# Attention on one core: the value block cut in two, and scores, score pieces and values put in another order

## The chip, the cores and the metric

The kernel runs on one core of a Trainium2 chip. The metric is the device time of one execution in microseconds. The time before is the median of three runs, and the profile is of one further execution with its own time.

## The reference

The input `x` has 2 batches of 2048 tokens with 256 channels. What is computed, cut to what matters:

```python
xn  = layernorm(x)
q, k, v = split(xn @ w_in.T)            # 16 heads of 16 channels
att = einsum('bhqd,bhkd->bhqk', q, k) / 4
att = where(causal, att, 0.0)           # masked scores are 0, not -inf
att = softmax(att)
x + (att @ v) @ w_out.T + ffn(xn)       # ffn: r * (relu(k)**2 @ W_v.T), token-shifted
```

A masked score is 0 and so still weighs its key with exp(0 - max). The kernel adds these keys by a term of their own, from sums of the values behind each query.

## The kernel before

**Stages.** `stage_tokens` normalises, projects and computes the feed-forward part, and lasts to about 222 us. `stage_attention` is the rest. It goes through 8 groups (2 batches by 4 groups of 4 heads). A group has 4 units (`u`, 512 queries each), and unit `u` has `4 * (u + 1)` key tiles (`kt`, 128 keys each): 40 steps in a group. In the last four steps of a unit (the diagonal) only the queries from `first_query` on count, so that these have 512, 384, 256 and 128 queries.

**One step of TensorE** (`group` of the tensor block, L1193) issues, in this order:

- four score tiles (`score_tile`, L1123; heads 0, 2, 1, 3). A head has 50 rows, and the heads lie alternately in rows 0 to 63 and 64 to 127 of the array. A score tile is called S0 to S3 here. S0 and S2 use the lower rows, S1 and S3 the upper.
- after S0 and after S2 one score piece each (`ops.score_piece`, L324): 128 queries by up to 512 keys of two heads, one matmul in the upper rows and one in the lower. VectorE reduces it to a maximum (`reduce_piece`, L349), for the softmax of a later unit. A piece on the diagonal is narrower (128 to 512 columns) and gets four small mask matmuls (L339). 32 of a group's 80 pieces are such. The pieces have two pairs of PSUM banks (`MRING`).
- after S1 `between_scores` (L1179): in step 1 the masked keys of the unit before (L1155, 32 small matmuls), in step 2 a suffix sum of the values (L1119, L1120), in the last group an output tile (L1175) in many steps.
- after S3 the value block of the key tile two steps earlier (`weigh_values`, L1133, `LAG` is 2): four heads in four column strips of the array, over all 128 rows, in fp32, which makes 8 matmuls in the trace. So step 0 of a unit has the values of the last unit's 256-query tile, step 1 those of its 128-query tile, step 2 those of this unit's tile 0, and the later ones those of its other tiles.

**What waits for what.** The score tiles take turns in three PSUM banks (`SRING` is 3, `bank_of`): the tile three uses later waits for ScalarE's exponential (L1014) of the tile before it in the bank. So S3 waits for the exponential of S0 of its own step. A piece waits for VectorE's reduction of the piece two before it. The values wait for the exponentials, and on the diagonal for GpSimd's mask (L966). Each engine takes its work in the order written out. The order of DMAs on the SP queue (L873) hangs on scores, values and reductions by semaphores and is not touched.

Of the kernel before, what the change touches and what calls it, by code (L numbers as in the profile page):

```python
# [18 lines left out]
CH = 512  # L19
NCH = T // CH  # L20
SUB = CH // P
NT = T // P
GH = 4
NG = H // GH
HW = 32
# [16 lines left out]
PIECE0 = [SUB * (GH // 2) * u * (u + 1) // 2 for u in range(NCH + 1)]  # L42
PIECES = PIECE0[NCH]
# [14 lines left out]
LAG = 2  # L58
NORM_AT = GH * LAG + 1
KT0 = [SUB * u * (u + 1) // 2 for u in range(NCH + 1)]  # L60
# [9 lines left out]
PRING = 16  # L70
SRING = 3
MRING = 2
# [11 lines left out]
def key_tiles(u):  # L84

    return SUB * (u + 1)


def first_query(u, kt):

    return P * max(0, kt - SUB * u)


def spread_pieces():
# [9 lines left out]
def pieces_at(u, kt, half):  # L104

    return SPREAD[u, kt, half], KT0[u] + kt >= AHEAD_FROM
# [14 lines left out]
def bank_of(what, which, G):  # L121

    return (G * len(score_uses()) + score_uses().index((what, which))) % SRING


def rows_of(h, rows):

    return slice(h // 2 * HALF, h // 2 * HALF + rows)
# [664 lines left out]
def stage_attention(nc, block, ops, stores, ident, attn_t, ffn_d, w_out_sb, out):  # L793
# [7 lines left out]
    with ExitStack() as ctx:  # L801
        def sb(name, shape, dt=F32):
            return ctx.enter_context(nc.sbuf_tensor(name, shape, dt))

        def ps(name, shape):
            return ctx.enter_context(nc.psum_tensor(name, shape, F32))

        def sem(name):
            return ctx.enter_context(nc.semaphore(name))

        probs = sb("probs", [P, PRING, CH])
# [8 lines left out]
        ps_m = ps("ps_m", [P, MBANKS, CH])  # L820
        ps_o = ps("ps_o", [P, CH])
# [3 lines left out]
        scores_ready, probs_ready, probs_masked, probs_used = (  # L825
            sem("scores_ready"), sem("probs_ready"), sem("probs_masked"), sem("probs_used"))
# [15 lines left out]
        q_op, k_op, v_sb, after, v_after = ops.q_op, ops.k_op, ops.v_sb, ops.after, ops.v_after  # L842
        keys_after, ones, row_max, shift_loaded, SHIFTS = ops.keys_after, ops.ones, ops.row_max, ops.shift_loaded, ops.SHIFTS
        front_loaded, back_loaded, after_ready, max_ready, shift_ready = (
            ops.front_loaded, ops.back_loaded, ops.after_ready, ops.max_ready, ops.shift_ready)
# [253 lines left out]
        def _(pe):  # L1099
            def wait_for_bank(what, which, i, p, first):  # L1100

                uses = score_uses()
                G = i * 2 + p
                at = uses.index((what, which)) - SRING
                if at < 0:
                    if not first:
                        pe.wait_ge(probs_ready, G * SLOTS + at + 1 + SRING)
                elif uses[at][0] == "scores":
                    pe.wait_ge(probs_ready, G * SLOTS + uses[at][1] + 1 + SRING)
                else:  # L1110
                    pe.wait_ge(v_after_ready, G * 4 + uses[at][1] + 1)
# [11 lines left out]
            def score_tile(u, kt, at, i, p, first, last):  # L1123

                slot = (KT0[u] + kt) * GH + at
                h = HEAD_AT[at]
                rows = rows_of(h, KROWS)
                q0 = first_query(u, kt)
                wait_for_bank("scores", slot, i, p, first)
                pe.matmul(ps_s[:, bank_of("scores", slot, i * 2 + p), 0:CH - q0], k_op[rows, p, h % 2, kt * P:(kt + 1) * P],  # L1130
                          q_op[rows, p, h % 2, u * CH + q0:(u + 1) * CH], start=True, stop=True).then_inc(scores_ready, 1)

            def weigh_values(p, u, kt, G):  # L1133

                n = G * NCH + u
                if kt == 0:
                    pe.wait_ge(sums_ready, n + 1)
                if kt < SUB * u:
                    pe.wait_ge(probs_ready, G * SLOTS + (KT0[u] + kt + 1) * GH + SRING)
                else:  # L1140
                    pe.wait_ge(probs_masked, n * (SUB * GH) + (kt - SUB * u + 1) * GH)
                q0 = first_query(u, kt)
                for at, h in enumerate(HEAD_AT):
                    last = pe.matmul(ps_o[h * HW:(h + 1) * HW, q0:CH], v_sb[:, p, kt, h * HW:(h + 1) * HW],  # L1144
                                     probs[:, ((KT0[u] + kt) * GH + at) % PRING, 0:CH - q0],
                                     start=(kt == 0), stop=(kt == key_tiles(u) - 1))
                last.then_inc(probs_used, 1)

            def masked_keys(p, u, G):

                pe.wait_ge(diag_ready, (G * NCH + u + 1) * DIAGS)
                pe.wait_ge(v_after_ready, G * 4 + u + 1)
                for s in range(SUB):
                    for h in range(GH):
                        last = pe.matmul(ps_o[h * HW:(h + 1) * HW, s * P:(s + 1) * P],  # L1155
                                         v_after[:, p, u * SUB + s, h * HW:(h + 1) * HW],
                                         diag_weight[:, u % 2, h * SUB + s], start=False, stop=False)
                last.then_inc(masked_done, 1)

            def finish_unit(p, u, G, step):  # L1160

                weigh_values(p, u, key_tiles(u) - LAG + step, G)

            def output_tile(k):

# [13 lines left out]
            def between_scores(i, p, u, kt, first, last):  # L1179

                G = i * 2 + p
                nxt = NCH if u == NCH - 1 else 0
                if kt == LAG - 1 and u > 0:
                    masked_keys(p, u - 1, G)
                elif kt == LAG - 1 and not first:
                    masked_keys(1 - p, NCH - 1, G - 1)
                if last and (u, kt) in OUT_AT:
                    output_tile(OUT_AT[u, kt])
                if (u, kt) in SV_AT:
                    wait_for_bank("suffix", SV_AT[u, kt], i, p, first)  # L1190
                    sum_suffix(p, SV_AT[u, kt], G, bank_of("suffix", SV_AT[u, kt], G))

            def group(i, p, first=False, last=False):  # L1193
                G = i * 2 + p
                if not first:
                    pe.wait_ge(front_loaded[p], ops.loaded(p, i + 1))
                    pe.wait_ge(back_loaded[p], ops.loaded(p, i + 1))
                for u in range(NCH):
                    nxt = NCH if u == NCH - 1 else 0
                    pe.wait_ge(shift_loaded[u % 2], (G * (NCH // 2) + u // 2 + 2) * SHIFTS)  # L1200
                    for kt in range(key_tiles(u)):
                        for at in range(GH):
                            score_tile(u, kt, at, i, p, first, last)
                            some, ahead = pieces_at(u, kt, at // 2)
                            if at % 2 == 0 and not (ahead and last):
                                for f in some:
                                    if ahead and f == 0:
                                        pe.wait_ge(front_loaded[1 - p], ops.loaded(1 - p, i + 1 + p))
                                    if ahead and f == PIECE0[NCH // 2]:
                                        pe.wait_ge(back_loaded[1 - p], ops.loaded(1 - p, i + 1 + p))  # L1210
                                    ops.score_piece(pe, ps_m, MRING, f, 1 - p if ahead else p, (G + ahead) * PIECES)
                            if at == GH // 2 - 1:
                                between_scores(i, p, u, kt, first, last)
                            if at == GH - 1:


                                if kt >= LAG:
                                    weigh_values(p, u, kt - LAG, G)
                                elif u > 0:
                                    finish_unit(p, u - 1, G, kt)  # L1220
                                elif not first:
                                    finish_unit(1 - p, NCH - 1, G - 1, kt)
                if last:
                    masked_keys(p, NCH - 1, G)
                    for step in range(LAG):
                        finish_unit(p, NCH - 1, G, step)
                    for k in range(len(OUT_AT), OUTS):
                        output_tile(k)

# [3 lines left out]
            pe.wait_ge(ops.piece_reduced, HEAD_START + MRING)  # L1233
            stores.gates(pe)
            group(0, 0, first=True)
            for i in range(B * CC - 1):
                group(i, 1)
                group(i + 1, 0)
# [29 lines left out]
```

## Time and profile before

| | |
|---|---|
| median of 3 runs | 1095.94 us (1093.55 to 1103.12) |
| profiled execution, own time | 1095.51 us |
| its span, first to last instruction | 1092.7 us |
| TensorE matmul busy (share of span) | 1051.1 us (96%) |
| VectorE busy | 843.1 us (77%) |
| ScalarE busy | 696.0 us (64%) |
| GpSimd busy | 386.3 us (35%) |
| exponentials (L1014) | 1280, 599.9 us busy |
| reductions of pieces (L349, ps_m) | 594, 612.0 us busy |
| value matmuls (L1144) | 2560, 301.8 us busy |

A busy TensorE is not one at its peak: the ends of matmuls are modelled, and two matmuls in different rows of the array overlap in the records. The start times are what is read. `PE` is TensorE's matmul, `PEld` its weight load, `ACT` ScalarE, `DVE` VectorE.

### The profile page before, as it was taken

Reading aid. Unit: us, or ns where it says so; the run is one execution under the profiler, and the core shown is the slowest. Engines: PE = TensorE matmul, PEld = TensorE weight load, DVE = VectorE, ACT = ScalarE, POOL = GpSimd, SP = SyncE. Lnnn points to the kernel's source line nnn. Section 1 sums busy time; section 2 is a strip of 40 time slices with the busy share of each in tenths; the row PEclk is TensorE's granted clock in tenths of the full one; section 3 lists DMA queues with packets and bytes.
Section 4 is the critical chain, followed back from the end, with each engine's and each line's share of the span. In section 5 each row is a group of like instructions: output and inputs, shape, how many; then the busy total and the mean of one; then the engine's idle time right before and its main releaser. Section 6 shows DMA issues by size and latency. Waiting matters only on the chain.

```text
span 1092.7 us, 21861 instructions
## 1 busy us (share of the span) xinstructions
PE 1051.1 (96%) x8064; PEld 535.8 (49%) x8064; DVE 843.1 (77%) x1185; ACT 696.0 (64%) x1487; POOL 386.3 (35%) x945
## 2 busy tenths in 40 slices
PE   5999999999999999999999999999999999999998
PEld 3655555554545454444444444544444445454445
DVE  4667788658889878987898889888988888898213
ACT  2433333247776777777777776777777777777672
POOL 3111211355314532445144424343532453163301
PEclk9999999969999999999999999999999999999999
DMA  3596664455004600460055026303520460002123
GB/s 119 171 270 183 192 215 148 145 80 101 8 9 64 103 7 8 65 107 3 16 101 66 7 29 101 47 7 48 94 36 7 60 107 8 9 20 71 45 82 121
DMA packets 62030, 84.13 MB, mean 77 GB/s; under 512 B 12260, under 2 KB 42212, under 8 KB 60900
## 3 DMA queue, kind: packets, MB, share of 16 engines
q1 hardware_dynamic: 60772, 78.55, 33.3%
q0 software_dynamic: 1152, 4.19, 1.3%
q8 instruction: 63, 1.03, 0.4%
q14 instruction: 43, 0.35, 0.1%
HBM read 44.30 MB, written 34.08 MB: 72 GB/s over the span
## 4 chain that ended last, share of the span: by engine, by line
PE 78%; DVE 15%; issue 3%; ACT 2%; DMA 1%; POOL 1%; SPq 0%; ACTq 0%; DVEq 0%; POOLq 0%
PE ps_s L1130 22%; PE ps_o L1144 22%; DVE part_max L349 10%; PE ps_m L332 9%; PE ps_vr L731 4%; PE ps_qk L722 3%; PE ps_o L1155 3%; PE ps_m L1175 3%; PE ps_m L339 3%; PE ps_xt L765 2%; ACT probs L1014 2%; PE ps_qk L731 2%; PE ps_s L1119 2%; DMA x_in<-x 1%; PE ps_s L1120 1%
## 5 line engine op out<-in xcount | busy, mean ns | idle before, releaser
L1014 ACT ACTIVATE probs<-ps_s 128x512 f32<-128x512 f32 (+3 forms) x1280 | 599.9, 537 | 232.4 <-PE ps_s L1130 226.2
L349 DVE TENSOR_REDUCE part_max<-ps_m 128x2 f32<-128x1024 f32 (+2 forms) x594 | 612.0, 1056 | 115.7 <-PE ps_m L332 89.2
L1130 PE MATMUL ps_s<-q_op,k_op 50*128 50x512 f32 (+3 forms) x1280 | 436.3, 424 | 7.0 <-ACT probs L1014 3.5
L332 PE MATMUL ps_m<-k_op,q_op 48*128 48x512 f32 (+3 forms) x1188 | 344.2, 412 | 13.8 <-DVE part_max L349 12.6
L1130 PEld LDWEIGHTS ps_s<-q_op,k_op 50*128 50x128 f32 x1280 | 208.7, 186 | 298.5 <-ACT probs L1014 228.0
L966 POOL TENSOR_SCALAR_AFFINE_SELECT probs<-probs 128x128 f32<-128x128 f32 x512 | 145.4, 294 | 448.3 <-ACT probs L1014 440.6
L1144 PE MATMUL ps_o<-probs,v_sb 128*32 128x512 f32 (+3 forms) x2560 | 301.8, 544 | 0.0
L332 PEld LDWEIGHTS ps_m<-k_op,q_op 48*128 48x128 f32 x1188 | 169.3, 187 | 41.0 <-DVE part_max L349 37.2
L933 POOL TENSOR_TENSOR diag_weight<-ident,masked_weight 128x256 f32<-128x256 f32 x256 | 150.3, 624 | 40.7 <-ACT masked_weight L987 40.6
L339 PE MATMUL ps_m<-mask,pick 64*128 64x64 bf16 (+1 forms) x932 | 97.7, 209 | 0.0
L1144 PEld LDWEIGHTS ps_o<-probs,v_sb 128*32 128x32 f32 x2560 | 50.6, 108 | 71.2 <-ACT probs L1014 33.8
L349 DVE TENSOR_REDUCE part_max<-ps_pieces 128x2 f32<-128x1024 f32 (+3 forms) x46 | 46.5, 1011 | 31.6 <-PE ps_pieces L339 17.7
L722 PE MATMUL ps_qk<-xn_t,w_in_sb 128*128 128x512 f32 x128 | 63.3, 625 | 1.9 <-issue 1.4
L663 ACT ACTIVATE parts<-ps_qk 128x512 fp32r<-128x512 f32 x32 | 19.1, 598 | 71.1 <-PE ps_qk L722 71.1
L523 POOL TENSOR_TENSOR k_act<-k_act 128x1024 f32<-128x1024 f32 x8 | 15.3, 1912 | 119.9 <-ACT k_act L688 119.9
L339 PEld LDWEIGHTS ps_m<-mask,pick 64*128 64x128 bf16 x932 | 47.1, 96 | 14.0 <-issue 1.2
L322 POOL TENSOR_TENSOR after<-after,v_sb 128x64 f32<-128x64 f32 x120 | 39.7, 331 | 8.8
L528 POOL TENSOR_TENSOR ffn<-ffn,x_in 128x512 f32<-128x512 f32 x16 | 21.5, 1346 | 49.8 <-DVE ffn L596 49.8
L722 PEld LDWEIGHTS ps_qk<-xn_t,w_in_sb 128*128 128x128 f32 x128 | 23.6, 196 | 26.0 <-issue 24.1
L1155 PE MATMUL ps_o<-diag_weight,v_after 128*32 128x128 f32 x1024 | 35.4, 280 | 0.0
L1175 PE MATMUL ps_m<-w_out_sb,attn_t 128*128 128x256 f32 x128 | 33.3, 397 | 0.0
L1155 PEld LDWEIGHTS ps_o<-diag_weight,v_after 128*32 128x32 f32 x1024 | 26.7, 111 | 11.7 <-POOL diag_weight L933 8.8
(76 smaller groups left out, 680.3 us busy)
## 6 DMA issues: line engine op xcount, KB each, us to landing
parts_d<-parts SPq DMA_DIRECT2D x32, 512.0 KB, 4.7
q_op<-parts_d SPq DMA_DIRECT2D x84, 128.0 KB, 8.0
k_op<-parts_d SPq DMA_DIRECT2D x84, 128.0 KB, 8.2
vpad_d<-v_pad SPq DMA_DIRECT2D x32, 256.0 KB, 3.5
v_sb<-vpad_d SPq DMA_DIRECT2D x8, 1024.0 KB, 5.8
x_in<-x SPq DMA_DIRECT2D x8, 512.0 KB, 4.9
ffn_d<-ffn SPq DMA_DIRECT2D x8, 512.0 KB, 3.2
attn_t<-normed SPq DMA_DIRECT2D x128, 32.0 KB, 2.0
```

The source lines that it names most:

```text
L332: last = pe.matmul(ps_m[:, f % ring * 2 + e, 0:width], self.q_op[rows, p, j, q0:q0 + P], self.k_op[rows, p, j, pc * CH:pc * CH + width], s ...
L339: last = pe.matmul(ps_m[:, f % ring * 2 + e, s * P + k * HALF:width], self.pick16[half, k], self.mask16[half, k, k * HALF:P], start=False, ...
L349: dve.tensor_reduce(both, ps_m[:, bank:bank + 2, 0:width], AX_X, ALU.max).then_inc(self.piece_reduced, 1)
L722: last = pe.matmul(ps_qk[:, j % 2], w_in_sb[:, cc, j * P:(j + 1) * P], xn_t[:, cc, 1:CH + 1], start=(cc == 0), stop=(cc == CC - 1))
L731: last = pe.matmul(psum[:, s], lhs[:, cc, t * P:(t + 1) * P], weights[:, cc], start=(cc == 0), stop=(cc == CC - 1))
L933: pool.tensor_tensor(diag_weight[:, u % 2, some], ident[:].unsqueeze(1).broadcast_to([P, GH * SUB // DIAGS, P]), masked_weight[:, u, some] ...
L966: pool.affine_select(out=blk, in_=blk, compare_op=ALU.is_ge, fill=0.0, base=0, pattern=[[1, P]], channel_multiplier=-1).then_inc(probs_mas ...
L1014: act.activation(probs[:, slot % PRING, 0:width], ps_s[:, bank_of("scores", slot, i * 2 + p), 0:width], ACT.Exp).then_inc(probs_ready, 1)
L1130: pe.matmul(ps_s[:, bank_of("scores", slot, i * 2 + p), 0:CH - q0], k_op[rows, p, h % 2, kt * P:(kt + 1) * P], q_op[rows, p, h % 2, u * CH ...
L1144: last = pe.matmul(ps_o[h * HW:(h + 1) * HW, q0:CH], v_sb[:, p, kt, h * HW:(h + 1) * HW], probs[:, ((KT0[u] + kt) * GH + at) % PRING, 0:CH ...
L1155: last = pe.matmul(ps_o[h * HW:(h + 1) * HW, s * P:(s + 1) * P], v_after[:, p, u * SUB + s, h * HW:(h + 1) * HW], diag_weight[:, u % 2, h ...
L1175: last = pe.matmul(ps_m[:, k % MBANKS, 0:C], attn_t[:, b * CC + cc, c * CH + t * P:c * CH + (t + 1) * P], w_out_sb[:, cc], start=(cc == 0) ...
```

## The change

The value block is cut into two parts by queries. Part 0 is the columns up to 256 and part 1 the columns from 256. A block of key tile 0, and one whose first query is 256 or later, stays whole and is part 1. The order of a step, which was S0, piece, S1, between, S2, piece, S3, values, is now read from the string `ORDER`: S0, S1, piece, between, values part 0, S2, S3, piece, values part 1. The semaphore that says that a block's probabilities are used is raised by part 1. The other engines' programs are the same.

```diff
+ORDER = "SSMXASSMB"
+
+def weighed_columns(u, kt, part):
+    q0 = first_query(u, kt)
+    if kt == 0 or q0 >= CH // 2:
+        return (q0, CH) if part == 1 else None
+    return (q0, CH // 2) if part == 0 else (CH // 2, CH)
...
-            def weigh_values(p, u, kt, G):
+            def weigh_values(p, u, kt, G, part):
                 n = G * NCH + u
+                if weighed_columns(u, kt, part) is None:
+                    return
...
                 q0 = first_query(u, kt)
+                q1, q2 = weighed_columns(u, kt, part)
                 for at, h in enumerate(HEAD_AT):
-                    last = pe.matmul(ps_o[h * HW:(h + 1) * HW, q0:CH], v_sb[:, p, kt, h * HW:(h + 1) * HW],
-                                     probs[:, ((KT0[u] + kt) * GH + at) % PRING, 0:CH - q0],
+                    last = pe.matmul(ps_o[h * HW:(h + 1) * HW, q1:q2], v_sb[:, p, kt, h * HW:(h + 1) * HW],
+                                     probs[:, ((KT0[u] + kt) * GH + at) % PRING, q1 - q0:q2 - q0],
                                      start=(kt == 0), stop=(kt == key_tiles(u) - 1))
-                last.then_inc(probs_used, 1)
+                if part == 1:
+                    last.then_inc(probs_used, 1)
...
                     for kt in range(key_tiles(u)):
-                        for at in range(GH):
-                            score_tile(u, kt, at, i, p, first, last)
-                            some, ahead = pieces_at(u, kt, at // 2)
-                            if at % 2 == 0 and not (ahead and last):
...
+                        at = m = 0
+                        for op in ORDER:
+                            if op == "S":
+                                score_tile(u, kt, at, i, p, first, last)
+                                at += 1
+                            if op == "M":
+                                some, ahead = pieces_at(u, kt, m)
+                                m += 1
+                                if not (ahead and last):
...
+                            if op == "X":
                                 between_scores(i, p, u, kt, first, last)
-                            if at == GH - 1:
+                            if op in "AB":
+                                part = "AB".index(op)
                                 if kt >= LAG:
-                                    weigh_values(p, u, kt - LAG, G)
+                                    weigh_values(p, u, kt - LAG, G, part)
```

## Rows read from the trace of the kernel before

**Rows 1.** Waits over the whole run: who waited for whom, us in total, times, longest

```profile
PEld ps_s L1130 <- ACT probs L1014: 228.0, 390, 1.3
PEld ps_m L332 <- DVE part_max L349: 37.2, 72, 0.8
```

**Rows 2.** Busy time by stretch, units 0 and 1: PE, PEld, DVE, ACT, POOL, clock, DMA

```profile
650.55:681.72 31.17, 30.10 (x292) 14.89 (x289) 28.76 (x37) 22.01 (x53) 13.84 (x41) 1.00 0.65 106
```

**Rows 3.** Timeline of one plain step: start us, length us, engine, line, operation [idle before]

```profile
630.44 0.50 PE L1130 MATMUL ps_s<-q_op,k_op 50*128 50x512 f32 x1
...
630.79 0.39 PE L1130 MATMUL ps_s<-q_op,k_op 50*128 50x512 f32 x1
...
631.02 0.39 PE L1130 MATMUL ps_s<-q_op,k_op 50*128 50x512 f32 x1
...
631.04 2.06 ACT L1014 ACTIVATE probs<-ps_s 128x512 f32<-128x512 f32 x4 [0.60 <-PE ps_s L1130]
631.22 2.36 DVE L349 TENSOR_REDUCE part_max<-ps_m 128x2 f32<-128x1024 f32 x2 [1.13 <-PE ps_m L332]
...
631.69 0.18 PEld L1130 LDWEIGHTS ps_s<-q_op,k_op 50*128 50x128 f32 x1 [0.48 <-ACT probs L1014]
...
632.12 1.06 PE L1144 MATMUL ps_o<-probs,v_sb 128*32 128x512 f32 x8
...
633.12 0.49 PE L1130 MATMUL ps_s<-q_op,k_op 50*128 50x512 f32 x1
```

**Rows 4.** Timeline, unit 2: end of step 0 and step 1

```profile
578.49 0.64 PE L1144 MATMUL ps_o<-probs,v_sb 128*32 128x256 f32 x8
...
579.06 0.50 PE L1130 MATMUL ps_s<-q_op,k_op 50*128 50x512 f32 x1
...
579.40 0.40 PE L1130 MATMUL ps_s<-q_op,k_op 50*128 50x512 f32 x1
...
579.73 1.08 PE L1155 MATMUL ps_o<-diag_weight,v_after 128*32 128x128 f32 x32
...
580.74 0.50 PE L1130 MATMUL ps_s<-q_op,k_op 50*128 50x512 f32 x1
...
581.41 0.42 PE L1144 MATMUL ps_o<-probs,v_sb 128*32 128x128 f32 x8
...
581.77 0.50 PE L1130 MATMUL ps_s<-q_op,k_op 50*128 50x512 f32 x1
```

**Rows 5.** Timeline, unit 2: step 2, its second piece 384 wide and masked

```profile
582.44 0.70 PE L1119 MATMUL ps_s<-v_sb,keys_after 128*128 128x256 f32 x2
...
583.50 0.50 PE L1130 MATMUL ps_s<-q_op,k_op 50*128 50x512 f32 x1
...
583.88 0.49 PE L1130 MATMUL ps_s<-q_op,k_op 50*128 50x512 f32 x1
...
584.30 1.06 PE L1144 MATMUL ps_o<-probs,v_sb 128*32 128x512 f32 x8
...
585.30 0.50 PE L1130 MATMUL ps_s<-q_op,k_op 50*128 50x512 f32 x1
```

**Rows 6.** Timeline: S0 of the first step of units 2, 3, 0, 1 and 2

```profile
576.49 0.49 PE L1130 MATMUL ps_s<-q_op,k_op 50*128 50x512 f32 x1
...
607.77 0.50 PE L1130 MATMUL ps_s<-q_op,k_op 50*128 50x512 f32 x1
...
650.56 0.49 PE L1130 MATMUL ps_s<-q_op,k_op 50*128 50x512 f32 x1
...
660.34 0.49 PE L1130 MATMUL ps_s<-q_op,k_op 50*128 50x512 f32 x1
...
681.72 0.50 PE L1130 MATMUL ps_s<-q_op,k_op 50*128 50x512 f32 x1
```

**Rows 7.** Timeline, last group: S2 and S3 as a couple without a piece, then values

```profile
1020.10 0.50 PE L1130 MATMUL ps_s<-q_op,k_op 50*128 50x512 f32 x2
...
1020.53 1.06 PE L1144 MATMUL ps_o<-probs,v_sb 128*32 128x512 f32 x8
```

More of the change, by code:

```diff
@@ L1158, in masked_keys, with finish_unit @@
                 last.then_inc(masked_done, 1)
-            def finish_unit(p, u, G, step):
-                weigh_values(p, u, key_tiles(u) - LAG + step, G)
+            def finish_unit(p, u, G, step, part):
+                weigh_values(p, u, key_tiles(u) - LAG + step, G, part)
             def output_tile(k):
@@ L1201, in group @@
                     for kt in range(key_tiles(u)):
-                        for at in range(GH):
-                            score_tile(u, kt, at, i, p, first, last)
-                            some, ahead = pieces_at(u, kt, at // 2)
-                            if at % 2 == 0 and not (ahead and last):
[L1206 to L1212, printed above, removed]
+                        at = m = 0
@@ new lines, in group @@
+                        for op in ORDER:
[6 more added lines that the diff above has]
+                                if not (ahead and last):
+                                    for f in some:
+                                        if ahead and f == 0:
+                                            pe.wait_ge(front_loaded[1 - p], ops.loaded(1 - p, i + 1 + p))
+                                        if ahead and f == PIECE0[NCH // 2]:
+                                            pe.wait_ge(back_loaded[1 - p], ops.loaded(1 - p, i + 1 + p))
+                                        ops.score_piece(pe, ps_m, MRING, f, 1 - p if ahead else p, (G + ahead) * PIECES)
+                            if op == "X":
@@ L1213, in group @@
                                 between_scores(i, p, u, kt, first, last)
-                            if at == GH - 1:
+                            if op in "AB":
+                                part = "AB".index(op)
                                 if kt >= LAG:
-                                    weigh_values(p, u, kt - LAG, G)
+                                    weigh_values(p, u, kt - LAG, G, part)
                                 elif u > 0:
-                                    finish_unit(p, u - 1, G, kt)
+                                    finish_unit(p, u - 1, G, kt, part)
@@ L1221, in group @@
                                 elif not first:
-                                    finish_unit(1 - p, NCH - 1, G - 1, kt)
+                                    finish_unit(1 - p, NCH - 1, G - 1, kt, part)
                 if last:
@@ L1225, in group @@
                     for step in range(LAG):
-                        finish_unit(p, NCH - 1, G, step)
+                        for part in range(2):
+                            finish_unit(p, NCH - 1, G, step, part)
                     for k in range(len(OUT_AT), OUTS):
```

## The prediction

> **What bounds the kernel now.** I read the timeline of one plain step first, then the table of waits, then the odd steps of a unit, then the starts of whole units.
>
> A plain step takes 2.68 us, from S0 at 630.44 to S0 at 633.12 [rows 3]. Four terms make it up, and they close a ring. S0's exponential starts 0.60 after S0, at 631.04. S3, which wants S0's bank, is let go 0.65 later, at 631.69. The value block follows at 632.12, 0.43 later, and the next S0 1.00 after that [rows 3]. TensorE has no other work before S3: S0 and its piece's first half, the second half and S1 at +0.35, S2 and half of the second piece at +0.58, the other half one couple (0.23) later, +0.81. From there to +1.25 it stands, 0.44 us. The table of waits shows the same over the run, 390 waits of score tiles for an exponential, 228.0 us in all [rows 1]. VectorE needs 2.36 of the step, ScalarE 2.06 [rows 3], so neither bounds a plain step, but both are near.
>
> **What TensorE's orders cost.** Matmuls in opposite row halves go in couples. From rows:
> - Couple behind couple: 0.23 (630.79 to 631.02) [rows 3].
> - The first couple behind a value block: 0.35 (630.44 to 630.79, and 579.06 to 579.40) [rows 3, 4], so 0.12 more.
> - From the start of the last couple to a block over all rows: 0.33 (579.40 to 579.73) [rows 4], so 0.10 more.
> - A value block, until the next score: 1.00 for 512 queries [rows 3], 0.57 for 256 (578.49 to 579.06), 0.36 for 128 (581.41 to 581.77) [rows 4]. Two of 256 cost 0.14 more than one of 512.
>
> So cutting a value block adds 0.14 + 0.12 + 0.10 = 0.36 us of TensorE per step, and one crossing each way. Against this stand 0.44 of standing still, and the lone S3's late load (its 0.43 instead of 0.33).
>
> The Trainium skill (TensorEngine Tiling (Array Packing), Key Properties) says that a change of tiling mode drains TensorE. It gives no price; the 0.10 and 0.12 above are this trace's price for it. If the drain cost nothing, 0.22 of each cut step would be saved, some 50 us of the forecast below.
>
> **The new steps.** A half step is a score couple, a piece couple, a value part: 0.35 + 0.33 + 0.57 = 1.25. A plain step is then 2.50, against 2.68. Does the ring allow it? S3 now starts 1.25 behind S0 at the earliest, and 0.60 + 0.65 = 1.25 is when the bank is free [rows 3]. It just fits. The next S1 wants the exponential of S2, by the same sum 1.25 after S2, and just fits too. VectorE's 2.36 fit in 2.50, and the pieces now come evenly, 1.25 apart, where they came 0.58 and 2.10 apart, so that a burst of its other work pushes TensorE less.
>
> That couples of two scores work is seen in the last group, where S2 and S3 start together and the values follow 0.43 later (0.12 + 0.23 + 0.10 gives 0.45) [rows 7].
>
> Now unit by unit, since the other steps don't gain:
> - **Diagonal steps.** Narrower scores don't shorten a couple that hides a load, and their exponentials were short, so that S3 hardly stood. They now pay 2.50. The last one, with a 384-query block cut 128 and 256, costs 0.35 + 0.33 + 0.36 + 0.35 + 0.33 + 0.57 = 2.29.
> - **Step 0.** Its block stays whole. S3 goes at 1.25 as before, but now the second piece is queued behind it: 1.25 + 0.35 + 0.33 + 0.57 = 2.50.
> - **Step 1.** 0.35 + 0.33, masked keys 1.01 (579.73 to 580.74) [rows 4], 0.35 + 0.33 + 0.36: 2.73. It was 2.71.
> - **Step 2.** The suffix comes at 0.67 and lasts 1.06, S3 goes at 2.11 (581.77 to 583.88) [rows 4, 5], held by S1's exponential as before. Behind it 0.35 + 0.33 + 1.00 give 3.79, against 3.53. In unit 0, where the scores are narrow, 0.68 + 1.06 + 0.35 + 0.33 + 1.00 = 3.42.
>
> Sums, against the lengths between the rows' starts [rows 6]:
> - unit 3: 2.50 + 2.73 + 3.79 + 12 x 2.50 + 2.29 = 41.31, was 42.79
> - unit 2: 9.02 + 8 x 2.50 + 2.29 = 31.31, was 31.28
> - unit 1: 9.02 + 4 x 2.50 + 2.29 = 21.31, was 21.38
> - unit 0: 2.50 + 2.73 + 3.42 + 2.29 = 10.94, was 9.78
>
> A group is 104.87 where it was 105.23: only the 18 plain steps gain, and nearly as much is given back.
>
> **Masked pieces.** Their four small matmuls were mostly under S3's standing. Now they end the piece couple that the value part waits for. The step of rows 5 prices them: with a 384-wide masked piece the block came 0.80 behind S2 (583.50 to 584.30) where a plain pair of couples takes 0.67 (580.74 to 581.41) [rows 4]. So 0.13 at 384 columns; at 0.05 per 128 columns (a quarter of 0.21) this is 0.18, 0.13, 0.08 and 0.03 for the four widths, mean 0.105. Some of it was already paid before, so I take 0.09. 32 such pieces in a group make 2.9 us. The bounds are 0 and 0.13, so 0 to 4.2 us. The group is then +2.5, seven groups +17.5.
>
> **The last group.** Its units 0 and 1 cost +1.1, their masks +0.8. From step 5 of unit 2 it has no pieces: three plain steps become 2.25 (S3 at 1.25, 0.43, 0.57), -0.42 each, -1.3. The 17 cut blocks in steps with an output tile pay the 0.14 of the cut and no more, since the output tile crosses anyway: +2.4. Sum +3.0.
>
> **At nothing.** The parts' semaphore waits: exponentials and masks of two steps earlier are long done. The later signal of used probabilities: four slots deep. The SP and GpSimd queues are as before, and their triggers move with the steps. VectorE's floor: units 0 and 1 hold 28.76 us of VectorE in 31.17 [rows 2]; they become 32.25, so it does not bind.
>
> **Sum.** The profiled execution took 1095.5 (its median of runs is 1095.94, so 0.4 off), plus 17.5 and 3.0 is 1116.0. I forecast 1115.
>
> **Rivals.**
> - **A, the masks are hidden, no change.** Mask matmuls run in one row half while the other still streams, and the 0.13 comes from one step where S3 was held as well. Then a group gives -0.36, and with the last group's +2.2 the time is 1095. TensorE's 37.2 us of waits for VectorE [rows 1], of which the even pieces may free more than I took, push the same way. Against: in rows 5 S3 itself went only 0.38 behind S2, 0.04 later than in a plain pair, so that most of the 0.13 came after it [rows 5]. Chance 0.28.
> - **B, a crossing costs less the second time.** If the new crossing cost half of its 0.36, 0.18 x 28 cut steps x 8 groups is 40 us less: 1075. It decides if value blocks overlap the couples' loads. Against: every block in the rows, wide or narrow, has the same fixed part: 1.00, 0.57 and 0.36 less their columns (0.86, 0.43, 0.21) leave 0.14 to 0.15 [rows 3, 4]. Chance 0.12.
> - **C, S3 breaks its couple.** Ring and order both come to 1.25. If the exponential of S0 ends even slightly later than 1.21 behind S0, S3 starts alone, its load bare, and the second piece, queued behind it, too. The price is 0.12 per cut step (the bare load), 0.12 x 28 x 8 = 27 us: 1142. It decides where ScalarE has other work in the step (the copy of sums, the weights). Chance 0.16.
> - **D, loads don't hide in the same half.** In the rows a load hides behind the couple ahead (0.23, not 0.35) [rows 3]. Were that lost where a piece follows the scores, each of 56 half steps would pay 0.12, 47 us in seven groups: 1162. The Trainium skill (TensorE: Matmul & The Clock Gate, The mechanism) says that a weight load overlaps a matmul in flight only where their row groups differ. The 0.23 speaks against it, for S2 came in the rows that the piece before it had used. Chance 0.04.
>
> My own case has 0.40. **Chances.** About 1% is what a measurement can tell from no change, here 1085 to 1107. Slower: nearly all of my case (0.38), C and D, 0.57. Same: A and the edges, 0.30. Faster: B, 0.13. The range runs from 1087, below A's 1095 by some waits for VectorE, to 1142, C. My case alone is 1105 to 1127 by the masks' bounds.
>
> **What would show it.** A plain step at 2.50 (630.44's successor) with S0 and S1 at one start; value parts of 0.57 at +0.68 and +1.93; fewer and shorter waits of scores for exponentials; the diagonal's last step near 2.29 against 1.79; step 2 near 3.79. The gap from a masked piece to the value part decides between me and A. S2 and S3 with different starts is C. I am wrong altogether if the half step is not 1.25.

## The result, and the profile after

The changed kernel takes 1084.07 us (median of 9, 1083.38 to 1088.56) against 1095.94 (9 runs). The ratio is 0.9898, with an interval of 0.9871 to 0.9925: 1% faster, small but clear of the noise. I had forecast 1115, slower, and a range from 1087.

The profiled execution took 1088.56, the longest of the nine, with a span of 1086.4. Its first masked keys come at 244.10, 2.3 us later than in the profile before; in the kernels below this moves between 239.9 and 244.5, whatever the edit, so that the comparisons go by single steps and by the groups behind it.

Part of this is the clock that TensorE was granted. The table of busy times has it at 0.50 (1.2 of 2.4 GHz) for 20.5 us from 226.1 on, where the attention stage has just begun:

```profile
226.10:246.60 20.50, 19.92 (x123) 10.30 (x123) 11.32 (x14) 9.12 (x23) 12.15 (x31) 0.50 0.74 109
```

In the 4.1 us ahead of it TensorE was busy for 1.9. The profile before has such a stretch of 17.1 us, and e2, e3 and e6 below have one of 6.8; all of them begin between 224 and 232 us. Of the nine runs the three with a mean granted clock of 0.997 took 1083.4 to 1084.5, the two with 0.991 1088.0 and 1088.6. So a few us between two runs can be the clock alone.

First the page, its chain that ended last, by engine and by line:

```profile
PE 86%; DVE 7%; issue 2%; ACT 2%; DMA 2%; POOL 1%; SPq 0%; DVEq 0%; ACTq 0%; POOLq 0%
```

It was TensorE 78% and VectorE 15%. Now the waits of the whole run that answer to [rows 1]:

```profile
PEld ps_s L1141 <- ACT probs L1025: 193.1, 483, 1.9
PEld ps_m L343 <- DVE part_max L360: 5.7, 17, 0.9
```

TensorE's waits for VectorE are down from 37.2 us to 5.7, with pieces that come 1.24 apart. The wait of the scores for an exponential has more entries and less time, and part of it is now the value part in front, which the table puts down to the exponential.

The timeline of a plain step, then three halves with masked pieces, answers to [rows 3]:

```profile
581.98 0.50 PE L1141 MATMUL ps_s<-q_op,k_op 50*128 50x512 f32 x2
582.32 0.40 PE L343 MATMUL ps_m<-k_op,q_op 48*128 48x512 f32 x2
...
582.65 0.64 PE L1158 MATMUL ps_o<-probs,v_sb 128*32 128x256 f32 x8
...
583.22 0.50 PE L1141 MATMUL ps_s<-q_op,k_op 50*128 50x512 f32 x2
...
584.46 0.49 PE L1141 MATMUL ps_s<-q_op,k_op 50*128 50x512 f32 x2
...
586.03 0.41 PE L343 MATMUL ps_m<-k_op,q_op 48*128 48x512 f32 x2
...
586.47 0.64 PE L1158 MATMUL ps_o<-probs,v_sb 128*32 128x256 f32 x8
...
587.38 0.23 PE L343 MATMUL ps_m<-k_op,q_op 48*128 48x128 f32 x2
587.45 0.26 PE L350 MATMUL ps_m<-mask,pick 64*128 64x128 bf16 x4
...
587.64 0.64 PE L1158 MATMUL ps_o<-probs,v_sb 128*32 128x256 f32 x8
```

A half step is 1.24 (581.98 to 583.22 to 584.46), 0.34 + 0.33 + 0.57, where 1.25 was forecast; a plain step is 2.48 where it was 2.68. S0 and S1 start together, and so do S2 and S3. A 512-wide masked piece puts the value part 0.44 behind it instead of 0.33; a 128-wide one, masks and all, 0.26.

The diagonal of unit 2 and its borders, where the forecast went wrong:

```profile
597.20 0.45 PE L1141 MATMUL ps_s<-q_op,k_op 50*128 50x384 f32 x2
597.48 0.40 PE L343 MATMUL ps_m<-k_op,q_op 48*128 48x512 f32 x2
...
599.49 0.39 PE L1141 MATMUL ps_s<-q_op,k_op 50*128 50x256 f32 x2
599.71 0.40 PE L343 MATMUL ps_m<-k_op,q_op 48*128 48x512 f32 x2
...
601.72 0.33 PE L1141 MATMUL ps_s<-q_op,k_op 50*128 50x128 f32 x2
601.88 0.44 PE L343 MATMUL ps_m<-k_op,q_op 48*128 48x512 f32 x2
...
603.77 0.50 PE L1141 MATMUL ps_s<-q_op,k_op 50*128 50x512 f32 x2
```

The second, third and fourth steps of the diagonal start at 597.20, 599.49 and 601.72, and the next unit at 603.77: 2.29, 2.23 and 2.05, not 2.50, 2.50 and 2.29. The piece follows two full scores after 0.34, 384-wide ones after 0.28, 256-wide ones after 0.22, 128-wide ones after 0.16.

By unit (stretches of the table of busy times, here of units 2, 3, 0 and 1) [rows 2, 6]:

```profile
572.98:603.77 30.79, 30.52 (x360) 14.58 (x356) 25.94 (x37) 24.16 (x51) 13.93 (x40) 1.00 0.39 48
603.77:645.13 41.36, 41.01 (x449) 18.19 (x445) 35.84 (x41) 32.81 (x68) 13.89 (x33) 1.00 0.03 7
645.13:655.46 10.33, 10.05 (x122) 5.23 (x118) 9.49 (x15) 6.71 (x18) 4.56 (x17) 1.00 1.03 129
655.46:676.39 20.93, 20.62 (x224) 9.57 (x220) 19.86 (x24) 15.45 (x35) 9.29 (x25) 1.00 0.44 94
```

The four make 103.41 where they made 105.23, so -1.8 a group. From the first to the last group's masked keys, seven groups, it is 726.3 before and 714.2 after, -12.1. The last group gives back 3.6: from its first masked keys to the end 124.55 became 128.13. Together this is 8.5 us, 0.8%. The medians are 11.9 apart; the profiles show no more than 8.5 of it as the new order's, and I take the rest for the clock.

By kind of step, in the mean of the six groups between the first and the last, the change takes 2.65 us off the 18 plain steps of a group and 0.76 off the second and third steps of the diagonals. It adds 0.20 to the four steps 0, 0.82 to the four steps 2 (13.79 to 14.61) and 0.75 to the four last steps (7.47 to 8.22). Steps 1 stay as they were. So it gives back half of what it gains.

### The profile page after: what moved, and what is told of

Its sections match the earlier page's. It is cut to its first block, busy times and chain, and to the rows that moved or that the text cites. A ratio compares the mean times of both kernels' runs of the same rounds, so it can differ in the third digit from the quotient of the medians.

```text
span 1086.4 us, 25445 instructions
## 1 busy us (share of the span) xinstructions
PE 1054.0 (97%) x9856; PEld 525.5 (48%) x9856; DVE 851.4 (78%) x1185; ACT 709.9 (65%) x1487; POOL 385.3 (35%) x945
## 4 chain that ended last, share of the span: by engine, by line
PE 86%; DVE 7%; issue 2%; ACT 2%; DMA 2%; POOL 1%; SPq 0%; DVEq 0%; ACTq 0%; POOLq 0%
PE ps_o L1158 27%; PE ps_s L1141 23%; PE ps_m L343 10%; PE ps_vr L742 4%; DVE part_max L360 3%; PE ps_qk L733 3%; PE ps_o L1170 3%; PE ps_m L350 3%; PE ps_xt L776 2%; PE ps_m L1190 2%; PE ps_qk L742 2%; PE ps_s L1130 2%; ACT probs L1025 2%; DMA x_in<-x 1%; PE ps_s L1131 1%
## 5 line engine op out<-in xcount | busy, mean ns | idle before, releaser
L1025 ACT ACTIVATE probs<-ps_s 128x512 f32<-128x512 f32 (+3 forms) x1280 | 609.6, 533 | 210.4 <-PE ps_s L1141 196.2
L360 DVE TENSOR_REDUCE part_max<-ps_m 128x2 f32<-128x1024 f32 (+2 forms) x594 | 619.7, 1060 | 97.0 <-PE ps_m L343 66.3
L1158 PE MATMUL ps_o<-probs,v_sb 128*32 128x256 f32 (+2 forms) x4352 | 349.9, 393 | 0.0
L1141 PE MATMUL ps_s<-q_op,k_op 50*128 50x512 f32 (+3 forms) x1280 | 330.2, 464 | 10.5 <-ACT probs L1025 9.6
L1141 PEld LDWEIGHTS ps_s<-q_op,k_op 50*128 50x128 f32 x1280 | 141.1, 185 | 271.2 <-ACT probs L1025 193.1
L343 PE MATMUL ps_m<-k_op,q_op 48*128 48x512 f32 (+3 forms) x1188 | 247.7, 376 | 1.0 <-DVE part_max L360 0.4
L1158 PEld LDWEIGHTS ps_o<-probs,v_sb 128*32 128x32 f32 x4352 | 86.1, 108 | 116.6 <-ACT probs L1025 48.6
L343 PEld LDWEIGHTS ps_m<-k_op,q_op 48*128 48x128 f32 x1188 | 125.0, 189 | 5.8 <-DVE part_max L360 5.7
L350 PE MATMUL ps_m<-mask,pick 64*128 64x128 bf16 (+1 forms) x932 | 75.5, 210 | 0.0
L350 PEld LDWEIGHTS ps_m<-mask,pick 64*128 64x128 bf16 x932 | 34.9, 96 | 33.9 <-issue 19.1
```

What stands on the lines that cost most here:

```text
L343: last = pe.matmul(ps_m[:, f % ring * 2 + e, 0:width], self.q_op[rows, p, j, q0:q0 + P], self.k_op[rows, p, j, pc * CH:pc * CH + width], s ...
L350: last = pe.matmul(ps_m[:, f % ring * 2 + e, s * P + k * HALF:width], self.pick16[half, k], self.mask16[half, k, k * HALF:P], start=False, ...
L360: dve.tensor_reduce(both, ps_m[:, bank:bank + 2, 0:width], AX_X, ALU.max).then_inc(self.piece_reduced, 1)
L1025: act.activation(probs[:, slot % PRING, 0:width], ps_s[:, bank_of("scores", slot, i * 2 + p), 0:width], ACT.Exp).then_inc(probs_ready, 1)
L1158: last = pe.matmul(ps_o[h * HW:(h + 1) * HW, q1:q2], v_sb[:, p, kt, h * HW:(h + 1) * HW], probs[:, ((KT0[u] + kt) * GH + at) % PRING, q1 - ...
```

## The experiments

Each is the changed kernel with one edit, unless it says otherwise. The order of a step is a string: S a score tile, M a piece, X what stands between, A and B the value parts, V the whole block. Ratios are to the kernel before, in runs on the same chip. "Seven groups" is the stretch from the first to the last group's masked keys in the profile: it leaves the start and the last group out. It begins in unit 1 of the first group and ends in unit 0 of the last, so that it is 10 us short of seven whole groups. e6 is the change itself up to the last group, and has 712.9 where the change has 714.2: a difference of 1.3 in this figure says nothing.

**e1_order_only**

```diff
-ORDER = "SSMXASSMB"
+"SSMXSSMV"      # V: the whole block
```

> Only the order: S0, S1, piece, between, S2, S3, piece, and the value block whole behind it. If the gain came from the order alone, this is as fast as the change, about 1084. By my terms it can't be: S3 still waits until 1.25 behind S0, and the second piece and the whole block are now queued behind it: 1.25 + 0.35 + 0.33 + 1.00 = 2.93 for a plain step against 2.68. 0.25 in 18 plain steps, some 0.25 in the diagonal's first two and in steps 0 and 2, make about 6.5 us a group: near 1145.

Measured: 1146.69, ratio 1.0492 (1.0422 to 1.0562); seven groups 772.9. As expected to 2 us, with plain steps of 2.90 to 3.01 in its profile where 2.93 was summed. The order without the cut is 5% slower, because S3 waits and everything stands behind it.

**e2_cut_only**

```diff
-ORDER = "SSMXASSMB"
+"SMSXSMSAB"     # the order before, both parts behind S3
```

> Only the cut: the order before, with both value parts side by side behind S3. The ring S0, exponential, S3, values is closed as before with 1.14 in place of 1.00: a plain step 2.82, 28 cut blocks a group, 0.14 each, 31 us in all: near 1127. If a cut block cost nothing of itself, 1096.

Measured: 1095.09, ratio 1.0031 (1.0001 to 1.0061); seven groups 726.3, as before. I had 1127. Timeline of its plain step:

```profile
636.50 1.07 PE L1161 MATMUL ps_o<-probs,v_sb 128*32 128x256 f32 x16
637.50 0.18 PEld L1143 LDWEIGHTS ps_s<-q_op,k_op 50*128 50x128 f32 x1 [0.41 <-ACT probs L1027]
```

Sixteen matmuls of 256 columns take the 1.00 that eight of 512 took. That both profiles have 726.3 is partly chance, since the one before has 3 us of half clock in it and e2 none; the five groups from the third on take 526.3 against 525.2. That is 0.2 a group where I had put 3.9. So the 0.14 is not a price of cutting. It is the third part of a crossing, paid once for each stay in the column strips. The sum of a half step was right, since it has one such stay. The 0.14 for an output tile's step was right too, since each part has a stay of its own there, but I had called it by the wrong name.

**e3_couples_before**

```diff
-ORDER = "SSMXASSMB"
+"SMSXASMSB"     # score and piece in a couple, as before
```

> The old couples with the cut between them: S0, piece, S1, between, part 0, S2, piece, S3, part 1. Theory 1 (what counts is that a half step holds two couples and half a block, 1.25): plain steps 2.48 as in the change; steps 0 and 2 keep their second piece ahead of the waiting S3 and stay at 2.4 and 3.5; but narrow scores share their couple with a full piece, so that the diagonal's steps are 2.5, 2.5, 2.3 and not 2.3, 2.2, 2.05. Group 102.6 without masks, near 1080. Theory 2 (the two scores side by side are what gains): near 1095. A masked piece is here followed by its scores, as in rows 5, and may cost up to 0.09 each, 20 us: then near 1100.

Measured: 1082.06, ratio 0.99 (0.9868 to 0.9932), no different from the change; seven groups 711.9 against 714.2. Theory 1 holds: what gains is a half block per half step, not which tiles lie side by side. Its plain steps without a masked piece take 2.48, as in the change. That the whole comes out the same is chance: in the mean of six groups its steps 0 and 2 are 1.6 a group shorter than the change's, and its plain and diagonal steps 1.4 longer. Its masked pieces, in the timeline:

```profile
622.53 0.50 PE L1143 MATMUL ps_s<-q_op,k_op 50*128 50x512 f32 x1
622.54 0.44 PE L345 MATMUL ps_m<-k_op,q_op 48*128 48x384 f32 x1
622.82 0.23 PE L352 MATMUL ps_m<-mask,pick 64*128 64x128 bf16 x1
622.87 0.34 PE L345 MATMUL ps_m<-k_op,q_op 48*128 48x384 f32 x1
...
623.32 0.64 PE L1161 MATMUL ps_o<-probs,v_sb 128*32 128x256 f32 x8
...
626.37 0.50 PE L1143 MATMUL ps_s<-q_op,k_op 50*128 50x512 f32 x1
...
627.22 0.64 PE L1161 MATMUL ps_o<-probs,v_sb 128*32 128x256 f32 x8
...
635.15 0.38 PE L1143 MATMUL ps_s<-q_op,k_op 50*128 50x256 f32 x1
...
635.71 0.64 PE L1161 MATMUL ps_o<-probs,v_sb 128*32 128x256 f32 x8
```

From the first score to the values a plain half has 0.66 to 0.67. With a masked piece 384 wide it has 0.79, 512 wide 0.85. These are the 0.13 and 0.18 of the prediction: the price was right for this order, where a score comes behind the piece, and wrong for the change, where the piece stands last. And with 256-wide scores the half has 0.56, though each score shares its couple with a full piece. I expected narrow scores to save nothing here; that was wrong too.

**e4_after_no_masks**

```diff
-                             ..., start=True, stop=(pc < u))
-        if pc == u:
+                             ..., start=True, stop=True)
+        if False:      # the four mask matmuls of a diagonal piece
```

> The changed kernel without the mask matmuls of the diagonal pieces (their maxima are over unmasked scores). The prediction priced a masked piece at 0.09, 2.9 us a group, which makes about 21 us with the last group's eight: near 1063. The trace after shows gaps from piece to values that are longer by 0.11, 0.04, 0.07 and shorter by 0.07, mean 0.04; but the narrow couples stay narrow without their masks, so leaving out gives back the whole 0.11 per piece only where nothing else holds the step. Theory now: the masks themselves cost about 0.10, and the narrow width had paid back 0.08 of it.

Measured: 1067.64, ratio 0.9766 (0.9712 to 0.982); seven groups 698.6, 15.6 less than with masks: 0.07 for each of 224 masked pieces. 1063 was too low by 5 us.

**e5_before_no_masks** (the same edit in the kernel before)

> The kernel before without the mask matmuls. If S3's standing covered them, as the prediction says, at most 3 us less than before: 1093 to 1096. If they were paid before as well, 10 or more less.

Measured: 1084.83, ratio 0.991 (0.9881 to 0.9939); seven groups 720.5, 5.8 less than with masks, 0.026 each. At most 3 us less was expected, so this missed: S3's standing covered most of the masks but not all. It covered them in the 18 plain steps of a group, which take 48.55 with and without; most of what they cost is in the four steps 0, 9.89 with and 9.36 without. In the change the plain steps take 45.90 with them and 44.90 without. The change adds the difference, 9.8 us in seven groups, 0.044 each; I had taken 0.09, which is 20. The medians by themselves can't size this: they put e4 16.4 and e5 10.0 below the same kernels with masks, each uncertain by some us.

**e6_last_group_before**

```diff
+"SMSXSMSV" if last and (u == 3 or (u == 2 and kt >= 8)) else "SSMXASSMB"
```

> The change, but steps with an output tile (last group, unit 3 and the diagonal of unit 2) in the order before with whole blocks. The trace after has 3.24 us for such a step where it was 2.92: 0.14 for the cut and 0.18 of S1 waiting for a bank. 20 steps at up to 0.32 less: 4 to 6 us below the change, near 1079. If only the cut costs there, 2.4 below.

Measured: 1081.72, ratio 0.9883 (0.9837 to 0.9929). Four runs don't tell this from the change, but the last group does: from its masked keys to the end 122.97, against 128.13 in the change, 5.2 less. Timelines of a step with an output tile, first the change's, then this one's:

```profile
1034.13 0.49 PE L1141 MATMUL ps_s<-q_op,k_op 50*128 50x512 f32 x2
1034.55 0.64 PE L1158 MATMUL ps_o<-probs,v_sb 128*32 128x256 f32 x8
1035.12 0.68 PE L1141 MATMUL ps_s<-q_op,k_op 50*128 50x512 f32 x2
1035.73 1.13 PE L1190 MATMUL ps_m<-w_out_sb,attn_t 128*128 128x256 f32 x4
1036.80 0.64 PE L1158 MATMUL ps_o<-probs,v_sb 128*32 128x256 f32 x8
1037.36 0.50 PE L1141 MATMUL ps_s<-q_op,k_op 50*128 50x512 f32 x2
```

```profile
1029.09 0.51 PE L1143 MATMUL ps_s<-q_op,k_op 50*128 50x512 f32 x2
1029.52 1.13 PE L1193 MATMUL ps_m<-w_out_sb,attn_t 128*128 128x256 f32 x4
1030.58 0.50 PE L1143 MATMUL ps_s<-q_op,k_op 50*128 50x512 f32 x2
1031.01 1.06 PE L1161 MATMUL ps_o<-probs,v_sb 128*32 128x512 f32 x8
1032.01 0.50 PE L1143 MATMUL ps_s<-q_op,k_op 50*128 50x512 f32 x2
```

3.23 (1034.13 to 1037.36) against 2.92 (1029.09 to 1032.01). In the change a couple without a piece is only 0.99 behind the one before, so that S1 (1035.12, the pair 0.68 long instead of 0.50) meets its busy bank: the ring, at 0.18 a step. The other 0.13 are the second stay in the strips.

**e7_last_diagonal_before**

```diff
+"SMSXSMSV" if kt == key_tiles(u) - 1 else "SSMXASSMB"
```

> The change, but the last step of each unit in the order before with its 384-query block whole. It was 1.79 before and is 2.05 in the change: 0.26 less, 32 times: 8 us, near 1076. If the crossing and the cut cost nothing there, no change, 1084.

Measured: 1078.82, ratio 0.9858 (0.9816 to 0.9899); seven groups 707.9, 6.3 less than the change and 5.0 less than e6, where 0.26 in 28 steps would be 7.3. As expected in kind, but not in every unit: the last steps of units 0 to 2 are 0.22 to 0.28 shorter, and unit 3's takes 2.10 where the change takes 2.06 (before's order has 2.11 there, not 1.79).

**e9_wide_scores**

```diff
-pe.matmul(ps_s[:, bank, 0:CH - q0], k_op[...], q_op[rows, p, h % 2, u * CH + q0:(u + 1) * CH], ...)
+pe.matmul(ps_s[:, bank, 0:CH],      k_op[...], q_op[rows, p, h % 2, u * CH:(u + 1) * CH], ...)
```

> The change with the diagonal's score tiles computed 512 queries wide (what lies before the first query is extra; exponentials and all else keep their widths and read the first columns, so that the scores they read are others). Prediction's step: narrow scores shorten nothing, the diagonal's steps are 2.50, 2.50 and 2.29 anyway: then no change, 1084. New theory: each row half is a queue of its own and pays the columns of its own matmuls, 0.053 us per 128; then 384, 256 and 128 wide scores saved 0.05, 0.11 and 0.13 per half step, and made wide they give back 0.11 + 0.21 + 0.26 = 0.58 per unit, 2.3 a group, 18 us: near 1102.

Measured: 1101.86, ratio 1.0053 (1.0023 to 1.0083): 18 us more than the change, as the new theory has it. In the profile it is less: seven groups 726.4, 12.2 more than the change and 13.5 more than e6, 1.9 a group where 2.3 was summed. Its diagonal, in the timeline:

```profile
603.32 0.50 PE L1141 MATMUL ps_s<-q_op,k_op 50*128 50x512 f32 x2
...
604.55 0.50 PE L1141 MATMUL ps_s<-q_op,k_op 50*128 50x512 f32 x2
...
605.77 0.50 PE L1141 MATMUL ps_s<-q_op,k_op 50*128 50x512 f32 x2
...
608.08 0.50 PE L1141 MATMUL ps_s<-q_op,k_op 50*128 50x512 f32 x2
```

Its third step is 2.45 and its last 2.31 (605.77 to 608.08), near the 2.50 and 2.29 that the prediction put down for the change. So this kernel, half a per cent slower than before, has the diagonal that I had forecast.

**e8_by_step, e10_step0_after, e11_piece_ahead_of_s3**: versions that pick the order by the step.

```diff
 # e8
+if kt in (0, 2) or kt == key_tiles(u) - 1 or (last and (u, kt) in OUT_AT): "SMSXSMSV"
+else: "SSMXASSMB"
 # e10: as e8, without kt == 0
 # e11: as e8, but "SSMXSMSV" for kt 0, 2 and the last
```

> Each step in the order that is the shorter for it: before's order in steps 0 and 2 (the block is whole there anyway, and the second piece isn't queued behind the waiting S3), in the last step of a unit, and in steps with an output tile; the change's in all others. Step 0 about 0.1 less, step 2 0.28 less, the last step 0.26 less, 4 of each in 8 groups: 20 us, and the last group 5: 25 below the change, near 1060. If VectorE bounds units 0 and 1, some 5 to 8 less of that: 1067.

> As e8, but step 0 in the change's order. In e8 step 0 took 2.63 where the change takes 2.46 to 2.59, the second piece waiting for VectorE ahead of S3. If that is VectorE's lag, 0.1 in 32 steps less than e8: 1067. If VectorE bounds units 0 and 1 as a whole (31 us with 29 of VectorE), the wait turns up a step later and it is e8's time, 1070.

> As e8, but steps 0, 2 and the last of a unit in a mixed order: S0, S1, piece, between, S2, piece, S3, whole block. The first piece comes 0.35 later than in e8, which loads VectorE more evenly, the second still isn't queued behind S3. By TensorE's sums alone the same as e8, 1070; if the lag of VectorE in step 0 came from the early first piece, 1066; if a couple of two scores behind the block delays S2 and so S3, up to 1075.

Measured: e8 1069.93, ratio 0.9767 (0.9734 to 0.98); e10 1070.84, 0.9752 (0.9717 to 0.9787); e11 1073.07, 0.9779 (0.9742 to 0.9815). All three beat both kernels, by 2.2 to 2.5% over before, and can't be told from each other. The e8 gain over the change is about 14 us by the medians and 18 between the two profiled executions, where 25 were summed, and moving step 0 about changed nothing. Of 2.5 a group summed for its steps, 1.6 came. Steps 2 gave 0.75 of 1.12, nothing of it in unit 0, where the scores are narrow. The last steps gave 0.72 of 1.04, nothing of it in unit 3. Steps 0 gave 0.14 of 0.4: those of units 0 and 3 are shorter than in the change, and those of units 1 and 2 are 0.2 longer. One of these, of unit 2, in the timeline, with VectorE's rows:

```profile
464.27 4.08 DVE L364 TENSOR_REDUCE part_max<-ps_m 128x2 f32<-128x1024 f32 x4 [0.26 <-PE ps_m L347]
...
465.35 0.50 PE L1145 MATMUL ps_s<-q_op,k_op 50*128 50x512 f32 x1
...
466.68 0.39 PE L347 MATMUL ps_m<-k_op,q_op 48*128 48x256 f32 x2 [0.37 <-DVE part_max L364]
```

Four reductions run without a gap, and the second piece of this step waits for them. Units 0 and 1, just ahead of it, hold 29.0 us of VectorE in 30.4 us by now (9.77 and 20.61). That what is saved in them returns as such a wait is my reading. e10 fits it: its units 0 and 1 take 30.5, with step 0 in the other order.

## Why the prediction was wrong, by its steps

**Right.** The ring and its terms: 0.60, 0.65, 0.43, 1.00, and e1 within 2 us of what they give. The half step: 1.25 forecast, 1.24 measured, the bank free just in time, with the crossing paid in full, which refutes rival B. The unsplit steps of units with full scores: step 0 2.46 to 2.59 (2.50), step 1 2.64 to 2.70 (2.73), step 2 3.82 to 3.84 (3.79). Rival C shows only behind a half step that is shorter than the ring's 1.25: after the 1.17 of the 128-wide piece the next pair of scores is 0.58 long instead of 0.50.

**Right by luck.** The last group, +3.6 for +3.0. Its units 0 and 1 cost 0.1 more than before where I had 1.9, by the errors below, and eleven of its steps with an output tile cost 0.31 to 0.33 more each where I had 0.14, since I had not put the ring's 0.18 in.

**The step that failed: "Narrower scores don't shorten a couple that hides a load."** I read couples as lock-step: both halves of the array start a pair together, and 0.35 is the least. In the profile before, the narrow S0 stood beside a 512-wide piece half, and S1 came behind that piece in the same rows of the array: its 0.34 was the piece's, not the load's. Its timeline has this in the third step of unit 2's diagonal:

```profile
603.75 0.38 PE L1130 MATMUL ps_s<-q_op,k_op 50*128 50x256 f32 x1
603.75 0.61 PE L332 MATMUL ps_m<-k_op,q_op 48*128 48x512 f32 x2
604.09 0.39 PE L1130 MATMUL ps_s<-q_op,k_op 50*128 50x256 f32 x2
```

The piece's two halves last 0.61 together, and 0.73 beside a 512-wide S0 (579.06): the one behind S0 starts 0.12 sooner there, the S1 behind the other does not. Each row half is a queue of its own, as long as the sum of its own matmuls. In the change the lower half has S0 and its piece half, the upper S1 and its, and a score 128 columns narrower ends the half step 0.05 to 0.06 sooner: 0.34, 0.28, 0.22, 0.16 to the piece. The three last steps of the diagonal, with unit 0's last, took 22.1 a group where I had 24.2, and unit 0's steps 1 and 2, narrow as well, 2.59 and 3.13 where I had 2.73 and 3.42: 2.5 a group, 17 us in the seven groups. e9 shows that it is the width, by making the scores wide: 18 us back by the medians, 12 to 14 in the seven groups. e3 shows that it is each half by itself: there narrow scores gain 0.10 beside full pieces, where a pair in lock-step would gain nothing. The Trainium skill (TensorEngine Tiling (Array Packing), Key Properties) says that tiles operate independently, loads and matmuls in parallel; the trace agrees, by the 0.12 above, and I had drawn on the sentence beside it and not on this one.

**The mis-sized term: the masks.** "At 0.05 per 128 columns this is 0.18, 0.13, 0.08 and 0.03" holds in e3's order, with a score behind the piece. With the piece last, the value part comes 0.11 later for 512 columns and 0.07 earlier for 128. The four halves from 585.12 on are 1.35, 1.17, 1.30 and 1.27, mean 1.27 against 1.24. That is 0.03 for a masked piece over a plain one where I took 0.09: 32 pieces, 1.9 a group, 13 us in the seven groups. e4 less e5 measures another thing, the masks alone, after less before: 0.044. Rival A (the masks hidden) is refuted by that: they cost more than before, by 9.8 us.

Both errors went the same way. For the seven groups I had +17.5, and the profiles have -12.1, 29.6 apart; the two make 17 and 13. The experiments split it in much the same way. Without masks the change gains 21.9 (720.5 to 698.6) where my steps had 2.5, 19 us; the masks add 9.8 where I had 20.2, 10 us. No rival had this mechanism; that the time lies between A's 1095 and B's 1075 is chance.

**The cut's own price** was put at 0.14 a block and is 0.00 in e2's row. In the half step this did no harm. **The drain:** the sentence on the Trainium skill (TensorEngine Tiling (Array Packing), Key Properties: a change of tiling mode drains TensorE) had 50 us less if the 0.10 and 0.12 for a crossing fell away. The crossing is 0.36 in all, and the measured half step has it in full, so the price by the rows was the right one. **Rival D** is refuted: a piece follows the scores of its own rows after 0.34 as in the couples before, so that its load is hidden. The sentence of the Trainium skill behind D (TensorE: Matmul & The Clock Gate, The mechanism: a load overlaps a matmul in flight only where their row groups differ) does not hold in this trace: in the step from 603.77 on the piece's loads start at 603.88, while a pair of scores (603.77, 0.50 long) takes both halves. **VectorE's standing** in unit 3 stayed: one half step is 1.65 (621.57 to 623.22), its piece held 0.39 by VectorE, and one soon behind it is 1.49, together 0.66 more than plain ones; I had let it go. That and the masks are why the 18 plain steps made 45.9, not 45.0.

## What to carry to other kernels

Sum up each row half of TensorE as a queue of its own, and take the longer; a gap read between two matmuls is a price only for the neighbours that it had there. When a resource ring and an engine's order give the same length, count what the order does in each kind of step: here a cut that gains 3.4 us a group in the plain and diagonal steps gave half of it back in steps 0 and 2, where the block is whole, and in the last step of a unit. Choosing the order by the kind of step gave 2.2 to 2.5% instead of 1%. And when 1% is at stake, look at the granted clock of both runs, and compare stretches at the same clock.

## What the runs showed of the hardware

Sixteen 256-column matmuls in four column strips take the same 1.00 as eight of 512: the fixed 0.14 belongs to a stay in that tiling. A stay of its own between row-half work costs 0.36 in all.

Matmuls in different row halves do not start in program order. In e3 a mask matmul (622.82) starts before a piece matmul (622.87) that stands before it in the program, and the same is in the kernel before (583.79 and 583.84).

A score tile that is late for its bank holds back what is queued behind it, in both halves, though in other cases the halves run apart: in the change's step 0 the second piece starts with the late S3 (605.02) and not before it. That a wait stands in the one instruction stream, and the row halves part only behind it, is my reading; no run took it apart.
